# Two unread products of the identity ahead of each half of the transposed scores, in the last attention unit

## What is computed

```python
scores = jnp.einsum('bhqd,bhkd->bhqk', q, k) * scale
sparsity = scores.max(axis=-1) - scores.mean(axis=-1)
_, top_idx = jax.lax.top_k(sparsity, U)          # U = 307 of 512 rows are kept
scores_sel = jnp.einsum('bhud,bhkd->bhuk', q_sel, k) * scale
attn = jax.nn.softmax(scores_sel, axis=-1)
out_sel = jnp.einsum('bhuk,bhkd->bhud', attn, v)
out = jnp.zeros_like(q).at[bi, hi, top_idx].set(out_sel)
return out @ Wo + bo
```

## Time and profile before

| | us |
|---|---|
| median of 3 runs | 1556.13 |
| lowest and highest | 1555.75, 1557.9 |
| the profiled execution, its own time | 1559.04 |
| its span in the trace | 1557.0 |
| TensorE busy | 1467.0 (94%) |
| VectorE busy | 1104.2 (71%) |
| ScalarE busy | 664.3 (43%) |
| GpSimd busy | 556.1 (36%) |

### The profile page before, as it was taken

One profiled execution on the slowest core, in us unless ns is written; L12 is line 12 of the kernel. 1 busy time (PEld: TensorE's weight loads), 2 busy tenths in 40 slices (PEclk: granted clock), 3 DMA queues, 4 the chain that ended last, 5 costly groups with the idle time before them and its releaser, 6 DMA issues.

```text
span 1557.0 us, 25479 instructions
## 1 busy us (share of the span) xinstructions
PE 1467.0 (94%) x8792; PEld 1047.6 (67%) x8840; DVE 1104.2 (71%) x2127; ACT 664.3 (43%) x971; POOL 556.1 (36%) x705
## 2 busy tenths in 40 slices
PE   8899999999997699999989899999999999999998
PEld 7444444444342478888868687878888787888787
DVE  6888888888888755555585877776867777775542
ACT  1577777777766232223334233323334333332211
POOL 6446555555450232123222322323332232331420
PEclk9899999999998799999999999999999999999999
DMA  4423323323230400101100001001010100100001
GB/s 117 110 57 76 71 56 70 74 62 67 60 73 2 139 28 28 41 28 50 41 14 28 14 1 41 1 15 27 0 40 0 28 13 1 40 0 14 14 1 27
DMA packets 56414, 61.04 MB, mean 39 GB/s; under 512 B 15733, under 2 KB 41637, under 8 KB 56349
## 3 DMA queue, kind: packets, MB, share of 16 engines
q1 hardware_dynamic: 42653, 43.89, 10.7%
q0 software_dynamic: 13408, 16.29, 4.9%
q10 hardware_dynamic: 288, 0.00, 0.0%
HBM read 25.51 MB, written 8.90 MB: 22 GB/s over the span
## 4 chain that ended last, share of the span: by engine, by line
PE 50%; issue 20%; DVE 14%; POOL 8%; ACT 4%; SPq 1%; DMA 1%; another core or an unknown queue 0%; POOLq 0%; DVEq 0%; ACTq 0%
PE ps L1963 14%; PE ps L1991 9%; PE ps L960 5%; PE ps L945 4%; PE ps L931 4%; PE ps L888 3%; POOL h L1566 3%; POOL kT L1539 2%; PE ps L1974 2%; DVE mc L632 2%; PE ps L1949 1%; PE ps L2003 1%; PE ps L898 1%; DVE race L731 1%; DVE top L730 1%
## 5 line engine op out<-in xcount | busy, mean ns | idle before, releaser
L632 DVE TENSOR_REDUCE mc<-ps 128x2 f32<-128x1024 f32 x256 | 305.4, 1220 | 47.3 <-PE ps L931 46.7
L1991 PE MATMUL ps<-w_hi,h 128*128 128x256 f32 x1024 | 220.0, 299 | 11.2 <-DVE h L1803 11.2
L1870 ACT ACTIVATE h<-ps 128x512 fp32r<-128x512 f32 x128 | 76.1, 598 | 315.1 <-PE ps L2021 198.8
L1991 PEld LDWEIGHTS ps<-w_hi,h 128*128 128x128 f32 x1024 | 166.7, 190 | 19.7 <-DVE h L1803 17.6
L346 POOL DMA_DIRECT2D k_st<-k_hi x256 | 124.2, 490 | 141.8 <-PE ps L945 75.7
L1803 DVE SCALAR_TENSOR_TENSOR h<-ps,h 128x512 fp32r<-128x512 f32 x128 | 87.8, 690 | 121.9 <-ACT h L1870 119.2
L1566 POOL TENSOR_TENSOR h<-hf,h 128x512 fp32r<-128x512 f32 x56 | 72.3, 1292 | 277.6 <-DVE h L1816 277.6
L1963 PE MATMUL ps<-xT_b,w_hi 128*128 128x512 f32 x512 | 167.5, 408 | 0.0
L1991 PE MATMUL ps<-w_lo,h 128*128 128x256 f32 x512 | 143.7, 281 | 0.0
L945 PE MATMUL ps<-q_st,k_st 64*128 64x512 f32 x512 | 122.6, 478 | 16.2 <-ACT pT1a L818 5.1
L945 PEld LDWEIGHTS ps<-q_st,k_st 64*128 64x128 f32 x512 | 48.5, 187 | 118.3 <-ACT pT1b L818 46.0
(11 more groups left out here) (276 smaller groups left out, 3439.4 us busy)
## 6 DMA issues: line engine op xcount, KB each, us to landing
q_st<-q_hi SPq DMA_DIRECT2D x256, 32.0 KB, 2.1
k_st<-k_hi POOLq DMA_DIRECT2D x256, 32.0 KB, 1.9
q_st<-q_lo SPq DMA_DIRECT2D x128, 32.0 KB, 2.0
k_st<-k_lo POOLq DMA_DIRECT2D x128, 32.0 KB, 1.9
x<-in_x_dram SPq DMA_DIRECT2D x8, 512.0 KB, 4.0
x_dram<-x SPq DMA_DIRECT2D x8, 512.0 KB, 2.9
yn<-x_dram SPq DMA_DIRECT2D x16, 256.0 KB, 3.7
x<-x_dram SPq DMA_DIRECT2D x16, 256.0 KB, 3.8
```

Of the source, the lines that this page charges most:

```text
L632: v.tensor_reduce(mc[par][:, qt, 2 * HU + j:MC:NPAIR], ps[:, at:at + 2, :], AX_X, ALU.max).then_inc(max_done, 1)
L1870: a.activation(h[s][m % 2][0][:, :], ps[:, RING[s] + m % 2, :], ACT.Relu).then_inc(F[s]["relu"], 1)
L1991: last = t_.matmul(ps[:, ACC[s] + t // 2, (t % 2) * D:(t % 2 + 1) * D], h[s][m % 2][a][:, t * P:(t + 1) * P], ws[k][:, m, :], start=m == 0 ...
```

## The change

A new entry `("busy",)` in the list of the last unit calls `keep_busy` with 2 products into bank 4, which no work of this unit uses. There are 12 entries, one ahead of each `("T", p, half)` from p = 1 on, so 24 products, without a wait of their own.

```diff
-    2 * B - 1: [("T", 0, 0), ("AV", 0), ("T", 0, 1), ("T", 1, 0), ("T", 1, 1), ("AV", 1), ("T", 2, 0), ("AV", 2),
-        ("T", 2, 1), ("T", 3, 0), ("T", 3, 1), ("T", 4, 0), ("AV", 3), ("T", 4, 1), ("T", 5, 0), ("O1",), ("O0",),
-        ("AV", 4), ("T", 5, 1), ("AV", 5), ("AV", 6), ("T", 6, 0), ("T", 6, 1), ("AV", 7)]}
+    2 * B - 1: [("T", 0, 0), ("AV", 0), ("T", 0, 1), ("busy",), ("T", 1, 0), ("busy",), ("T", 1, 1), ("AV", 1),
+        ("busy",), ("T", 2, 0), ("AV", 2), ("busy",), ("T", 2, 1), ("busy",), ("T", 3, 0), ("busy",), ("T", 3, 1),
+        ("busy",), ("T", 4, 0), ("AV", 3), ("busy",), ("T", 4, 1), ("busy",), ("T", 5, 0), ("O1",), ("O0",),
+        ("AV", 4), ("busy",), ("T", 5, 1), ("AV", 5), ("AV", 6), ("busy",), ("T", 6, 0), ("busy",), ("T", 6, 1),
+        ("AV", 7)]}
...
+                elif what == "busy":
+                    keep_busy(nc, bank[BUSY], ident, 2)
```

## The result

The changed kernel takes 1559.49 us (median of 20 runs, 1558.09 to 1561.3), the kernel before 1556.93 (median of 20 runs, 1555.75 to 1558.88). The ratio is 1.0013, 95% interval 1.0007 to 1.0019, so about 2.0 us slower, 1.1 to 3.0. That is still within 0.2%, as forecast, but the interval excludes zero, so it is a cost, and the time lies outside the range of 1554.7 to 1558.3. The profiled execution took 1559.34 us, its span is 1557.4. That is only 0.3 us more than the profiled execution of before, since this one reached the choice of the rows 1.03 us sooner, ahead of every added product; the cost is read from the medians, and in the traces from distances.

What follows compares the result with a forecast made beforehand. VectorE's choice of the rows, 26 rounds at 1.525 us, bounds the stretch. Three exposed pairs (1.41 us) plus 0.3 of remainders nearly fit the cover: +0.1 us, 1556.2 from a median of 1556.13, range 1554.7 to 1558.3.

Steps and rivals of the forecast that it cites:

- The price of a pair: Two identity products on TensorE: 0.47 us at full clock, 0.94 at half; twelve pairs 5.6 us.
- Which pairs are exposed: Walk through TensorE's and ScalarE's lists in the last unit: 1.41 us exposed and 0.3 us of remainders.
- three of twelve: Exposed pairs, those ahead of (T, 2, 0), (T, 2, 1) and (T, 6, 0), 0.47 us each, 1.41 together.
- the two pairs of step 1: Pairs in a half's 0.89 us wait for an exponential; at 0.47 each they leave nearly nothing, 0.1 to 0.2.
- What is in hand: Lateness allowed before the chain moves: 1.24 us by the second reciprocal, about 1.0 at the transposes of sel.
- The tail at full clock: From the products of step 7 to the last copy into oa, clock still full; chain cost 0 to 0.1 us.
- The rival with the tail at half clock: Clock half from 513.13 on as before: chain 1.2 us longer, 1557.4; chance 0.14.
- the filled pauses: TensorE's pauses of 1.00 and 1.80 us ahead of 513.13 mostly filled, so the half clock comes a few us later.
- The rival "TensorE becomes the bound": Cover gone, all 12 pairs on the path: 5.6 us less 1.0 to 1.24 in hand, +4.4, 1560.5; chance 0.04.
- The threshold that I had named: The rival of TensorE as bound decides from 1.0 us of lateness, and reaches 0.2% (3.1 us) at 4.2 us.
- my own estimate of 1.7: Lateness in us ahead of the products of step 7, which start at about 514.3 instead of 512.55.
- Downstream: Behind the unit: SyncE's loads 0.3 us later, priced at 0; half clock meets the transposes at 520 as before, no gain.

Runs made afterwards that it cites:

- the second trace: The changed kernel run once more with no edit, for a second trace; +1.9 us (0.5 to 3.3) on the kernel before.
- the nine-pair kernel: The changed kernel without the pairs ahead of (T, 2, 0), (T, 2, 1) and (T, 6, 0); +0.6 us (-0.8 to 2.0) on the kernel before.
- the changed kernel with the longer choice: The changed kernel with five more searches in the middle of VectorE's choice; +3.6 us (2.2 to 5.0) on the kernel before, 1561.09 us.
- the one with three pairs: The changed kernel with only the pairs ahead of (T, 2, 0), (T, 2, 1) and (T, 6, 0); +1.6 us (0.2 to 3.0) on the kernel before.
- the five in the waits: Changed kernel with pairs only ahead of (T, 1, 1), (T, 5, 0), products of step 6, and two ahead of step 7; 0.0 us (-1.4 to +1.4) on before.
- the kernel before with the longer choice: The kernel before with five more searches in the middle of VectorE's choice; +4.4 us (2.5 to 6.2) on the kernel before, 1562.14 us.
- the five pairs with filled gaps: Five pairs in TensorE's waits, 8 products behind the transposes of sel, 17 ahead of the second tokens' first transposes; 0.0 us (-1.4 to +1.4) on before.

## Why the prediction was wrong

- **The price of a pair** is the step that failed: 0.47 us, "and no other bound". What the runs showed in its place is 0.64 at all twelve entries. The 0.47 was read from the earlier trace rows, where a full-height product (L888) follows the pair. The same view has pairs with a product of part height behind them, 48 rows, which is what a half of the scores (64 rows) is near to. One of them:

```profile
41.36 0.71 PE L74 MATMUL ps<-ident 128*128 128x128 f32 x4
42.01 0.49 PE L931 MATMUL ps<-k_st,q_st 48*128 48x512 f32 x2
```

  That is 0.65 us. The nearest row for a price is one with the same follower, not only with the same instruction. Twelve pairs are 7.7 us and not 5.6.
- **Which pairs are exposed.** The way of finding them was right: with 0.64 it gives 3.3, and the second trace has 3.35, the nine-pair kernel 1.42 for 1.37, the kernel with four products 8.5 for 8.3. But exposure was read as a property of a place, three of twelve. It depends on the price: at 0.64 the two pairs of step 1, 1.28 us, no longer fit into 0.89 us of waiting, and what is left over from them reaches (T, 2, 0). (At 0.47 the two are 0.94, so they leave 0.05 over and not the 0.1 to 0.2 of the forecast; that doesn't change the sum.)
- **What is in hand** was right: 1.24 at the second reciprocal, 1.0 at the transposes. The full clock at the tail gives back another 0.7: from the products of step 7 to the end of the copy into `oa` it is 3.60 us before and 2.88 now. The lateness of 3.35 less 1.24 and 0.7 is the 1.4 of the second trace; the first adds its late start and the half clock up to 492.8, is 4.15 late and has 2.2.
- **The tail at full clock** came as forecast: full until 520.13 and, in the second trace, until 518.01, `sel` transposed in 0.60 in both. The rival with the tail at half clock didn't occur. The Trainium skill, TensorE: Matmul & The Clock Gate, section Why this matters for your kernels, lays a fall of the clock to a long gap; the trace of before doesn't agree, since the fall at 513.13 came behind no pause over 1.80 us, and taken as it stands that rule would have had no fall there at all. The reason that the forecast gave, the filled pauses, isn't shown. For it: the full stretch was 27.3 us in all three traces with 12 pairs of full height, 34.1 with four products an entry, and 20.5 in the two of before. Against it: it was 23.9 in the two other traces whose list for the unit has no pair at all, as it was with nine pairs, with one product and with half height. The later fall bought less than the 1.11 to 0.60 of the transposes of `sel`, since `selT` waits for the reciprocal and not for them; what it bought is the 0.7 us on the way there.
- **The rival "TensorE becomes the bound"** is what happened, at a point below its price: I asked for all twelve pairs on the path, +4.4 us, and gave it 0.04. The threshold that I had named, 1.0 us of lateness, was 0.7 below my own estimate of 1.7, which only the clock's help at the tail covered. With that help 1.94 us are in hand (1.24 and 0.7), 0.2 more than the estimate; a price read from one row and taken twelve times has more error than that. Twelve pairs at 0.2 us more are 2 us of work, and 1.6 of them came through.
- **Downstream.** From `selT` to the first h of the next part it is 29.80 and 29.20 us in the two traces of the changed kernel, 28.97 and 28.94 in those of before: 0.2 to 0.8 us more, beside the half stretches around 520 and 534. I had booked nothing for it. It isn't shown to belong to the change: the changed kernel with the longer choice has 28.94, the one with four products 28.48, and the one with three pairs 29.83.

## What to carry to other kernels

Work that is "hidden" by another engine's chain is hidden up to a number; write it down, and hold every estimate of lateness against it, with its own error times the count of insertions. Take the price of an instruction from a row in which the same kind of instruction follows. And if filler has to go in, put it ahead of the instruction that waits anyway, in a shape that leaves room for its neighbours. Here no filler gained time clear of the noise, so the first question is whether it has to.

## What the runs showed of the hardware

- A float32 product of the 128 x 128 identity ahead of one that uses 64 rows costs about 0.2 us once, besides 0.22 a product at full clock: 0.42, 0.64 and 1.09 us for 1, 2 and 4. Ahead of a product of 48 rows the pair was 0.65, ahead of one of full height 0.47. If the product itself takes 64 rows, its records interleave with the half's and the 0.2 us go: 0.44 for the pair.
- The clock fell to half in the middle of the unit in the trace of the three pairs (505.65 to 509.06) and in that of the five in the waits (502.54 to 512.78). It didn't in the six traces with twelve entries, but neither in the four whose list for the unit has no entry, nor in that of the nine, nor in the second with the five in the waits. So the entries aren't shown to guard against anything: in what share of the executions it happens, one or two traces of a kernel don't tell.
- Executions of one kernel differ in where the half stretches lie: the stretch ahead of the unit was 10.2 us with another of 3.4 behind it in both traces of before, 17.1 in one piece in the first of the changed kernel, in that of the three pairs, in that of the kernel before with the longer choice and in that of the five pairs with filled gaps. It comes with kernels of both sides. The program is the same up to there, and still the choice began anywhere from 473.8 to 477.0 us of the span.
